# An exchange of K's first block moved ahead of two loads of x on the queue of SyncE

## The reference, cut to what matters

```python
q = proj(x, Wq); k = proj(x, Wk); v = proj(x, Wv)        # x: (8, 512, 1024), 16 heads of 64
q = q * jnp.minimum(cond_1, 4.0)
scores = jnp.einsum('bhqd,bhkd->bhqk', q, k) / np.sqrt(HEAD_DIM)
scores = jnp.where(causal, scores, jnp.finfo(scores.dtype).min)
attn = jax.nn.softmax(scores, axis=-1)
out = jnp.einsum('bhqk,bhkd->bhqd', attn, v)             # then back to (8, 512, 1024)
y = jnp.einsum('bsd,ed->bse', out, Wo)
# y is quantised per row, the ffn weight to three values
return x + (jnp.einsum('bsi,oi->bso', q_y, q_w) + bias)
```

## Time and profile before

| | us |
|---|---|
| Median of 3 runs | 2128.12 |
| Lowest and highest | 2113.1 and 2131.9 |
| The profiled execution, its own time | 2122.68 |
| Its span, first to last instruction | 2120.6 |
| PE busy in the span | 1970.7 (93%) |
| Mean granted share of the TensorE clock | 0.97 |

### The profile page before, as it was taken

One profiled execution on the slowest core, in us unless ns is written; L12 is line 12 of the kernel. 1 busy time (PEld: TensorE's weight loads), 2 busy tenths in 40 slices (PEclk: granted clock), 3 DMA queues, 4 the chain that ended last, 5 costly groups with the idle time before them and its releaser, 6 DMA issues.

```text
span 2120.6 us, 40315 instructions
## 1 busy us (share of the span) xinstructions
PE 1970.7 (93%) x12378; PEld 1718.5 (81%) x12378; DVE 1365.3 (64%) x3331; ACT 1027.0 (48%) x2495; POOL 907.7 (43%) x984
## 2 busy tenths in 40 slices
PE   8999888799998999998998999999986999999998
PEld 6787667789888998987988988998985777777775
DVE  6545664477788777777666688767776545545454
ACT  4443333467677676776666667766775000000000
POOL 1333443244455444455444455444443444444442
PEclk9999999899999999999999999999997999999999
DMA  6899997877767778677577577677663333332322
GB/s 208 333 371 341 348 361 288 290 232 272 260 204 295 257 249 279 220 278 262 190 247 256 210 262 257 220 270 252 241 235 90 124 109 106 101 118 90 119 89 79
DMA packets 165696, 477.83 MB, mean 225 GB/s; under 512 B 12768, under 2 KB 84448, under 8 KB 135776
## 3 DMA queue, kind: packets, MB, share of 16 engines
q1 hardware_dynamic: 165072, 476.11, 64.7%
q10 hardware_dynamic: 528, 0.52, 0.1%
HBM read 331.88 MB, written 111.15 MB: 209 GB/s over the span
## 4 chain that ended last, share of the span: by engine, by line
PE 69%; DMA 11%; DVE 9%; issue 5%; ACT 3%; POOL 1%; SPq 1%; DVEq 0%; ACTq 0%; POOLq 0%
PE proj_ps L209 19%; PE s_ps L571 8%; PE proj_ps L571 8%; DMA k_sw<-k_st 7%; PE t_ps L985 6%; PE o_ps L373 5%; PE o_ps L642 5%; PE t_ps L335 5%; PE o_ps L985 4%; PE s_ps L295 3%; PE s_ps L296 2%; DMA xv_raw<-xT 2%; DVE k_st L276 2%; DVE pt_all L359 1%; DVE q_st L272 1%
## 5 line engine op out<-in xcount | busy, mean ns | idle before, releaser
L209 PE MATMUL proj_ps<-parts 128*128 128x256 f32 x5376 | 775.5, 293 | 6.6 <-DMA parts<-x_scratch 6.6
L209 PEld LDWEIGHTS proj_ps<-parts 128*128 128x128 f32 x5376 | 684.9, 194 | 17.0 <-DVE k_sum L244 6.5
L325 POOL TENSOR_TENSOR prob<-prob,row_inv 128x128 f32<-128x128 f32 (+3 forms) x512 | 372.5, 728 | 644.3 <-DVE row_inv L319 643.3
L313 ACT ACTIVATE prob<-prob,row_min 128x128 f32<-128x128 f32 (+3 forms) x512 | 287.6, 562 | 209.8 <-DVE row_min L307 205.2
L359 DVE TENSOR_TENSOR pt_all<-t_ps,pt_all 128x128 fp32r<-128x128 f32 (+3 forms) x512 | 249.3, 487 | 117.7 <-ACT pt_all L352 117.5
L307 DVE CUSTOM_DVE_ANT_0 prob<-s_ps,mask 128x128 f32<-128x128 f32 (+3 forms) x512 | 247.2, 483 | 44.3 <-PE s_ps L296 20.0
L335 PE MATMUL t_ps<-ident,prob 128*128 128x128 f32 x1280 | 234.3, 282 | 26.9 <-DVE pt_all L359 22.1
L295 PE MATMUL s_ps<-k_sw,q_st 128*128 128x128 f32 (+3 forms) x512 | 172.7, 337 | 75.8 <-DMA k_sw<-k_st 45.9
L627 ACT ACTIVATE yt_q<-t_ps 128x1024 bf16<-128x1024 bf16 x32 | 32.8, 1024 | 426.6 <-PE t_ps L620 426.6
L352 ACT ACTIVATE pt_all<-t_ps 128x128 fp32r<-128x128 f32 (+3 forms) x512 | 217.0, 424 | 15.3 <-PE t_ps L335 13.7
L335 PEld LDWEIGHTS t_ps<-ident,prob 128*128 128x128 f32 x1280 | 153.1, 143 | 53.6 <-issue 28.6
(11 more groups left out here) (124 smaller groups left out, 2796.5 us busy)
## 6 DMA issues: line engine op xcount, KB each, us to landing
parts<-x_scratch SPq DMA_DIRECT2D x224, 1024.0 KB, 7.5
x_scratch<-xv SPq DMA_DIRECT2D x112, 512.0 KB, 5.7
k_sw<-k_st SPq DMA_DIRECT2D x128, 256.0 KB, 4.1
xv_raw<-xT SPq DMA_DIRECT2D x17, 1024.0 KB, 8.8
v_scratch<-v_tmp SPq DMA_DIRECT2D x64, 256.0 KB, 5.2
v_raw<-v_scratch SPq DMA_DIRECT2D x32, 512.0 KB, 3.9
oT_scratch<-o_sum SPq DMA_DIRECT2D x64, 256.0 KB, 3.4
o_raw<-oT_scratch SPq DMA_DIRECT2D x32, 512.0 KB, 4.6
```

The lines of the kernel that those rows point to most:

```text
L209: mm = pe.matmul(qk_bank(w, m), wc[w][:, c, wp, k, :], xq[:, c, :, xp, k, :], start=(fresh and k == 0 and i == 0), stop=(k == CH - 1 and i ...
L313: act.activation(prob[u % QT], prob[u % QT], ACT.Exp, bias=row_min[:, u % 4:u % 4 + 1], scale=-1.0, accum_out=row_sum[:, u % 4:u % 4 + 1]) ...
L325: pool.tensor_tensor(prob[u % QT], prob[u % QT], row_inv[:, u % 4:u % 4 + 1].broadcast_to([P, w]), ALU.mult).then_inc(norm_done, 1)
```

## The change

In `sp_step` the exchange of K's first block of `now` is issued between load P6 and load P5 and no longer behind load P7. Nothing else is edited.

```diff
             if nxt:
                 load_xq(sp, nxt[0], nxt[2], M_P6)
+            if now:
+                swap_k(sp, now[0], 0)
+            if nxt:
                 load_xq(sp, nxt[0], nxt[2], M_P5)
                 load_xq(sp, nxt[0], nxt[2], M_P7)
-            if now:
-                swap_k(sp, now[0], 0)
```

## The result

The changed kernel takes 2065.05 us (median of 4 runs, 2064.83 to 2065.57) against 2129.28 us (median of 4 runs of the kernel before, 2113.1 to 2131.9). The ratio is 0.9714, with a 95% interval of 0.9666 to 0.9763. The profiled execution took 2065.57 us, with a span of 2063.6, so 57.1 us less than the profiled execution of before. The forecast was 56.5 us less, and 2067 us.

What follows compares the result with a forecast made beforehand. PE, busy 93% of the span, was taken to bound the kernel. Waits 37.8, clock 21.7 and first item 4, less 7 for later loads, took 56.5 us off 2122.7, giving 2066.2; forecast 2067 us, range 2050 to 2084, chance 0.66.

Steps and rivals of the forecast that it cites:

- That the exchange's issue would not move, and only its company would: SP's queue: the exchange still issues as VectorE ends; without loads in flight it lands at 843.0, not 845.0.
- my 4.5: Upper end of the sign for being right: the exchange's second DMA lands 3.7 to 4.5 us after issue.
- The feared share of P5: DMA engines: P5, following 0.6 us behind the exchange, may take a share at its end; landing taken as 843.0, not 842.2.
- the rival of a half slowed exchange: Loads issued behind still slow the exchange, half of the delay stays, 37 us gained, 2086 us; chance 0.18.
- The waits of S(0): PE's 23 second-phase waits for K's exchange, 45.9 us, shrink to 0.35 us each for the row minimum: 37.8 us gained.
- The clock: PE's granted clock falls behind nine of the longer waits; without those waits, all 21.7 us are gained.
- The first item: PE's 11.5 us wait before the first item's S(0) shrinks by 4 us, between 0 and 6.1.
- The later loads: The one cost: P5, P7 and P3 land later, with 0.8 to 1.4 us in hand; 0.3 us a step, 7 us lost.
- S(0) starts at about 844.0: In the step read, with the exchange down by 843.7, the row minimum ends S(0)'s wait; it had started at 845.23.
- all that follows on PE is 1.2 us earlier: PE's work behind S(0) in the step, K's products included, moves forward by the same 1.2 us.
- The sum: 37.8 + 21.7 + 4 - 7 = 56.5 us off the profiled 2122.7 gives 2066.2; against the median 2071.6.
- The low end of the range: No loss to the loads and 6.1 us at the first item, 2057, less 10 us for run spread; range stated from 2050.

Runs made afterwards that it cites:

- e3: Kernel before, order unchanged, with loads P5 and P7 inside the steps bringing 128 KB in place of 1 MB: 2067.45 us, ratio 0.9732.
- e1: Kernel before with only load P7 moved behind the exchange of K's first block, P5 still ahead: 2070.54 us, ratio 0.9749.
- e4: Changed kernel with the first of VectorE's two instructions for Q's low part moved ahead of L(10): 2047.42 us, ratio 0.9641 to the kernel before.
- e2: Kernel before with the exchange of K's first block ahead of P6, P5 and P7, so P6 leaves late too: 2127.29 us, ratio 1.0007.

## Why the prediction was right, point by point

**That the exchange's issue would not move, and only its company would.** Right. SP issues it at 818.51, as VectorE ends, and its second DMA lands 3.8 us after issue, against 3.7 for one with nothing beside it and my 4.5. e3 shows the same landing with the old order, and e1 with P5 still ahead. The feared share of P5, issued 0.85 us behind the second DMA, is not seen. So the rival of a half slowed exchange (0.18) had been given too much. The Trainium skill (DMA: Bandwidth & Descriptors, section Queues, rings and completion order) says that each DMA engine takes descriptors in the order of its ring; the prediction drew from this that nothing issued behind should delay the exchange, and the trace agrees, within 0.1 us.

**The waits of S(0).** Forecast 37.8 us. Measured: 45.9 + 14.9 before, 22.0 after, so 38.8 us. Two slips inside it nearly cancel. At 919.32 and 1284.25 the row minimum, late in steps with new weights, keeps 1.68 us of the wait and not 0.35. And two waits of 2.09 and 2.14 us for the row minimum (at 1361.83 and 1400.74), which the prediction let stay, fell to 0.27 and 0.35; what had made them long is open.

**The clock.** Forecast 21.7 us from nine stretches. In the changed kernel the clock is 1.00 from 388.8 to 1528 us, so these are gained, and so are three more (0.76 each) that I had left out, since S(0)'s waits of 1.7 to 1.8 us there stay nearly as they are. What a stretch costs is read from whole steps, S(0) to S(0). First before, with a clock of 0.57 for 7 us, then the same step of the changed kernel:

```profile
1084.41 0.47 PE L295 MATMUL s_ps<-k_sw,q_st 128*128 128x128 f32 x1 [3.27 <-DMA k_sw<-k_st]
1125.58 0.47 PE L295 MATMUL s_ps<-k_sw,q_st 128*128 128x128 f32 x1 [3.24 <-DMA k_sw<-k_st]
```

```profile
1049.66 0.33 PE L295 MATMUL s_ps<-k_sw,q_st 128*128 128x128 f32 x1 [0.36 <-DVE row_min L307]
1085.71 0.33 PE L295 MATMUL s_ps<-k_sw,q_st 128*128 128x128 f32 x1 [0.36 <-DVE row_min L307]
```

The step took 41.17 us and takes 36.05. Of the 5.12 us, 2.88 are the longer wait at the end (3.24 - 0.36). The other 2.24 are what the clock cost, less the 0.49 us that the second wait behind S(0) costs now (below): so 2.7 us for the clock, where 0.43 x 7 = 3.0 was forecast. Worked out in this way from the starts of S(0) in all steps, the five long stretches cost 13.5 us (forecast 15.0), the four short ones 6.2 (forecast 6.7; one of these steps now holds a late load of 1.35 us, which is set apart), and the three left out 1.9, where the missing share alone would say 0.24 x 7 = 1.7 each. The term is 21.6 us, as forecast. That is partly luck: nine stretches were counted a little too dear, and three were missing. Why the three cost so little was not looked into.

**The first item.** Forecast 4 us; its wait went from 11.5 to 4.8, 6.7 us. That is more than the 6.1 us of the two loads' own bytes, the upper end of the forecast; why is open.

**The later loads.** Forecast 7 us, measured 2.2 in three waits, the longest 1.4. P5 took 6.7 us from issue and not 7.9, so it landed at 826.6, with 2.2 us in hand and not 0.8. P3 left 2.5 us behind the second DMA of the exchange and not 1.6 us as reckoned (0.9 as before, and 0.7 for the two issues ahead), and took 10.6 us. It landed at 832.1, 0.9 us ahead of the product that needs it, in the second half of the first row below. So P3 had the least in hand, about the 0.8 us of the forecast. P4, the last load, took 11.6 us instead of 9.1; it landed at 835.3, 1.3 us ahead of its product in the second row:

```profile
832.20 1.68 PE L209 MATMUL proj_ps<-parts 128*128 128x256 f32 x12
836.61 1.68 PE L209 MATMUL proj_ps<-parts 128*128 128x256 f32 x12
```

**The step that was missing.** "S(0) starts at about 844.0" and "all that follows on PE is 1.2 us earlier" was wrong by half a microsecond. From S(0) to K's third product it is 825.42 - 824.50 = 0.92 us, and before it was 845.66 - 845.23 = 0.43, by this row of PE's timeline before and the S(0) of the earlier trace rows:

```profile
845.66 0.96 PE L209 MATMUL proj_ps<-parts 128*128 128x256 f32 x6
```

The transposes between them need VectorE's next instruction, L359, which ends 0.69 us behind the row minimum. While PE stood for the exchange, VectorE had got to it. The difference, 0.49 us here, lies between 0.33 and 0.49 in 22 of the steps (where the clock was lowered before, its 0.43 of full clock is taken). One step, at 502.15, had 0.92 us before, and those with waits of 1.7 us for the row minimum do not change. In all, 10.4 us are given back. e4 confirms it by removing the first wait and a part of the second at once.

**The sum.** The stretch from the first item's S(0) to the last one's took 1194.9 us and takes 1146.8 (384.01 to 1530.85): 48.1 us less. By terms: 38.8 + 21.6 - 10.4 - 2.2 = 47.8. With 6.7 us at the first item and 2.4 us that the first phase, which the change does not touch, happened to be shorter in this execution, the 48.1 come to 57.2; 0.3 us of the stretch stay open. So the total agreed with the forecast to 1 us in part by luck. The 10.4 us that were not in the sum were made up by loads priced 4.8 us too high, 2.7 too little at the first item, 1.0 too little for the waits, and the 2.4 us of the first phase; the clock's term was right to 0.1 us. That 2067 us stood so near to the median of 2065.05 is luck too: the sum itself gave 2071.6 against the median of before. The low end of the range was also miscounted, 2057 less 10 being 2047 and not 2050, which changes nothing here.

## What to carry to other kernels

When a transfer that PE waits for is issued the moment its data is ready and still lands late, look at what was issued in the microseconds before it and when that is needed: a load with slack that leaves after the urgent transfer costs nothing until the slack is used up, and the slack is a number to work out for each load (here 2.2 us for P5 and 0.9 for P3; with P6 late as well it was used up, and the whole gain was lost). When a wait goes, look at the other conditions of the waiting instruction and at the next two instructions behind it, since the engine that had time to catch up during the wait now has it no longer. An edit on that engine was worth about 8 us before the change and 18 after it.

## What the runs showed of the hardware that was not expected

The granted clock did not follow from single waits alone. Behind waits of 1.7 to 1.8 us it fell in three steps of the kernel before (the last of them in the first window below), and in none of the changed kernel, where waits of 1.68 us stand in the same steps. Behind the wait of 2.77 us at 429.33 it did not fall (second window). In e1, which has as few pauses as the changed kernel, it fell once, behind a wait of 1.68 us (third window), and e3 shows the same. And in e2, with waits no longer than 1.7 us behind the first item, it still fell in places. Why is left open; what can be said is that in these profiles fewer pauses in all went with fewer stretches of a lowered clock.

```profile
1284.20:1291.20 7.00, 6.78 (x40) 6.45 (x41) 6.07 (x17) 4.48 (x14) 4.24 (x7) 0.76 0.60 248
...
429.30:436.30 7.00, 6.97 (x54) 6.82 (x55) 3.26 (x12) 3.31 (x11) 3.42 (x5) 1.00 0.54 220
```

```profile
644.00:651.00 7.00, 5.53 (x31) 5.26 (x32) 6.54 (x18) 3.45 (x10) 3.57 (x5) 0.76 0.95 352
```

The Q instructions on VectorE (L272, two of them) take 1.52 us together in a plain step. In the first step with new weights they take 2.77 us, with GpSimd at work on sums of 128x512 beside them. The two rows are from the changed kernel, DVE and POOL at the same time:

```profile
597.19 2.77 DVE L272 SCALAR_TENSOR_TENSOR q_st<-q_sum,q_scale,q_st 64x512 fp32r<-64x512 f32 x2
```

```profile
597.67 1.74 POOL L446 TENSOR_TENSOR w_raw<-w_raw 128x512 f32<-128x512 f32 x1
```

The row minimum stands behind these instructions, so it is 1.3 us later there, and the exchange, early or late, did not touch those waits. Whether GpSimd's work is the cause of the longer time was not tried.
